# The last pass of a three-way product in 64-row halves, two chunks at a time, in the expert stage of a vision block

## What is computed

```python
logits = jnp.einsum('td,ed->te', xt, router_w)
probs = jax.nn.softmax(logits, axis=-1)
topk_w, topk_idx = jax.lax.top_k(probs, TOP_K)
topk_w = topk_w / jnp.sum(topk_w, axis=-1, keepdims=True)
comb = comb.at[jnp.arange(T)[:, None], topk_idx].add(topk_w)
for e in range(NUM_EXPERTS):           # 16 experts, 8 of width 128, 8 of width 256
    h = jax.nn.gelu(xt @ w1[:, off:off + wd])
    out = out + comb[:, e:e + 1] * (h @ w2[off:off + wd, :])
```

## Time and profile before

| | us |
|---|---|
| median of three runs | 736.07 |
| the profiled execution | 739.34 |
| its span in the trace | 737.6 |
| PE busy | 680.3 |
| VectorE busy | 496.5 |
| ScalarE busy | 356.3 |
| GpSimd busy | 108.2 |

### The profile page before, as it was taken

The page is one execution under the profiler, slowest core; times in us unless marked ns, Lnnn a source line. Parts: engine busy times, 40 slices in busy tenths (PEclk is TensorE's granted clock), DMA queues, the critical chain, the costliest instruction groups (busy, mean ns, idle before and its releaser), DMA issues.

```text
span 737.6 us, 30455 instructions
## 1 busy us (share of the span) xinstructions
PE 680.3 (92%) x13218; PEld 595.5 (81%) x13218; DVE 496.5 (67%) x1354; ACT 356.3 (48%) x921; POOL 108.2 (15%) x328
## 2 busy tenths in 40 slices
PE   5668999999999999999999999869999999999996
PEld 2457888788888888888888878748898898998986
DVE  5257778777878878877778877447456546646644
ACT  0125664655655655555555655534334344434432
POOL 0122123123123123223123211110000000000000
PEclk9969999999999999999999999979999999999999
DMA  8951111011011011111000000000000000000000
GB/s 311 300 182 60 61 48 44 33 44 48 33 60 33 32 60 32 32 61 32 32 4 5 4 4 4 4 1 2 1 1 21 0 0 21 0 0 21 0 0 22
DMA packets 12244, 30.48 MB, mean 41 GB/s; under 512 B 1120, under 2 KB 7392, under 8 KB 11616
## 3 DMA queue, kind: packets, MB, share of 16 engines
q1 hardware_dynamic: 12128, 28.73, 11.9%
HBM read 27.16 MB, written 1.57 MB: 39 GB/s over the span
## 4 chain that ended last, share of the span: by engine, by line
PE 76%; DVE 14%; ACT 5%; issue 3%; DMA 1%; POOL 1%; DVEq 0%; ACTq 0%; SPq 0%; POOLq 0%
PE ps L364 24%; PE ps L493 17%; PE ps L484 15%; PE ps L263 6%; DVE uu L734 3%; DVE sq L653 2%; PE ps L277 2%; PE ps L382 2%; PE ps L314 2%; DVE rf L741 2%; ACT qq L557 2%; PE ps L448 2%; PE ps L278 1%; ACT rr L561 1%; PE ps L375 1%
## 5 line engine op out<-in xcount | busy, mean ns | idle before, releaser
L884 DVE SCALAR_TENSOR_TENSOR acc<-ps,comb,acc 128x192 f32 x256 | 89.2, 411 | 90.3 <-PE ps L493 90.3
L493 PE MATMUL ps<-w_sb,work 128*128 128x192 f32 x768 | 139.9, 326 | 0.5 <-ACT work L633 0.3
L364 PE MATMUL ps<-rr 64*64 64x64 f32 x3840 | 131.4, 221 | 6.0 <-issue 3.3
L493 PEld LDWEIGHTS ps<-w_sb,work 128*128 128x128 f32 x768 | 129.2, 189 | 9.5 <-issue 1.7
L364 PEld LDWEIGHTS ps<-rr 64*64 64x64 f32 x3840 | 119.8, 136 | 18.7 <-ACT rr L561 10.6
L557 ACT ACTIVATE qq<-ps 128x384 f32<-128x384 f32 x192 | 92.3, 490 | 66.7 <-PE ps L364 64.7
L734 DVE SCALAR_TENSOR_TENSOR uu<-rr,qq 128x384 f32<-128x384 f32 x160 | 87.9, 559 | 50.8 <-ACT qq L557 44.6
L633 ACT ACTIVATE work<-ps 128x512 f32<-128x512 f32 x96 | 57.3, 597 | 133.6 <-PE ps L484 133.6
L561 ACT ACTIVATE rr<-ps 128x384 f32<-128x384 f32 x160 | 73.9, 490 | 80.6 <-PE ps L364 79.8
L364 PE MATMUL ps<-uu,qq 64*64 64x64 f32 x4608 | 96.6, 224 | 16.1 <-DVE uu L734 13.9
L364 PEld LDWEIGHTS ps<-uu,qq 64*64 64x64 f32 x4608 | 80.6, 134 | 33.9 <-DVE uu L734 30.6
(11 more groups left out here) (136 smaller groups left out, 1026.8 us busy)
## 6 DMA issues: line engine op xcount, KB each, us to landing
xtb<-xt_dram SPq DMA_DIRECT2D x16, 512.0 KB, 3.5
work<-x_dram SPq DMA_DIRECT2D x16, 512.0 KB, 3.4
wsh<-ws_dram SPq DMA_DIRECT2D x2, 1440.0 KB, 7.8
w_sb<-w_dram SPq DMA_DIRECT2D x1, 2304.0 KB, 26.3
w_a<-w_dram SPq DMA_DIRECT2D x1, 1536.0 KB, 13.2
w_b<-w_dram SPq DMA_DIRECT2D x2, 768.0 KB, 17.7
out_dram<-acc SPq DMA_DIRECT2D x4, 384.0 KB, 2.7
mult<-copies_dram SPq DMA_DIRECT2D x1, 512.0 KB, 12.8
```

Of the source, the lines that this page charges most:

```text
L364: last = pe.matmul(ps[z:z + 64, 2 * lane + i, 64 * j:64 * j + 64], lhs[r, lane, i, j, :], rhs[r, lane, i, j, :], start=True, stop=True)
L493: last = pe.matmul(ps[:, 2 + 2 * (e % 2) + j // 2, (j % 2) * DIM:(j % 2 + 1) * DIM], hid[:, c % 4, j * P:(j + 1) * P], w2_sb[:, c, :], sta ...
L884: last = dve.scalar_tensor_tensor(out=a, in0=ps[:, 2 + 2 * (e % 2) + j // 2, (j % 2) * DIM:(j % 2 + 1) * DIM].unsqueeze(1), scalar=comb[:, ...
```

## The change

Chunks are numbered through all groups, n from 0 to 95, and the loops over groups are written out on all engines. PE takes chunks in pairs. For a pair, `up_full` makes the first four passes of n, then of n + 1; then `up_half` makes the fifth pass of each on 64 rows: rows 0 to 63 for an even n, rows 64 to 127 for an odd one. The half used is the one where `wb` still holds the high part, so `low_part` now overwrites rows 64 to 127 for an even n and 0 to 63 for an odd one. The fifth pass has so far also had low part by xlo on the other half; this product is no longer computed. PE's order is up_pair(0), then up_pair(n + 2), down(n), down(n + 1). The up banks are three, 6, 0 and 1 (`UPB`); the weight slots are four (`SLOTS`), filled four chunks ahead; the memory for them comes from `wsh` and `whalo`, which only the start of the kernel uses. ACT's order per pair is two gelus, then two `high_part`; DVE's is two `low_part`, then the adds of the experts that end in the pair. `high_part` and `low_part` of four chunks instead of two stand ahead of `iteration(16)`.

```diff
+FIRST = [sum(WIDTH[:e]) for e in range(EXPERTS)]
+EXPERT_OF = [e for e in range(EXPERTS) for _ in range(WIDTH[e])]
+NC = NT // GT * HID
+UPB = (6, 0, 1)
+SLOTS = 4
...
-        wah, wal, wb = (sb(n, [P, 3, P], F32R) for n in ("wah", "wal", "wb"))
+        with nc.sbuf_tensor("wsh", [P, 2, 5, 3, DIM], F32) as wsh, nc.sbuf_tensor("whalo", [P, 2, DIM], F32) as whalo:
+            pass
+        wah, wal, wb = (sb(n, [P, SLOTS, P], F32R) for n in ("wah", "wal", "wb"))
...
+            def up_full(n):
+                g = n // HID
+                pe.wait_ge(whi_ready, 2 * n + 2)
+                pe.wait_ge(wlo_ready, 2 * n + 2)
+                if n >= 3:
+                    pe.wait_ge(gelu_done, n - 2)
+                tok4, k = slice(g * GT * P, (g + 1) * GT * P), n % SLOTS
+                parts = ((wah, xhi, 0), (wah, xlo, 0), (wal, xhi, 0), (wb, xhi, 1))
+                for m, (w, xs, half) in enumerate(parts):
+                    pe.matmul(ps[:, UPB[n % 3], :], w[:, k, :], xs[:, half, tok4], start=(m == 0), stop=False)
+
+            def up_half(n):
+                g, r = n // HID, slice(64 * (n % 2), 64 * (n % 2) + 64)
+                tok4 = slice(g * GT * P, (g + 1) * GT * P)
+                pe.matmul(ps[:, UPB[n % 3], :], wb[r, n % SLOTS, :], xlo[r, 1, tok4], start=False, stop=True).then_inc(up_done, 1)
+
+            def up_pair(n):
+                up_full(n)
+                up_full(n + 1)
+                up_half(n)
+                up_half(n + 1)
...
+            up_pair(0)
+            for n in range(0, NC, 2):
+                if n + 2 < NC:
+                    up_pair(n + 2)
+                down(n)
+                down(n + 1)
...
             act.wait_ge(ffw_loaded, 64)
-            high_part(0)
-            high_part(1)
+            for n in range(4):
+                high_part(n)
             iteration(NT)
...
+            for n in range(0, NC, 2):
+                gelu(n)
+                gelu(n + 1)
+                for m in (n + 4, n + 5):
+                    if m < NC:
+                        high_part(m)
...
-            low_part(0, 0)
-            low_part(0, 1)
+            for n in range(4):
+                low_part(n)
             iteration(NT)
...
+            for n in range(0, NC, 2):
+                for m in (n + 4, n + 5):
+                    if m < NC:
+                        low_part(m)
+                for m in (n, n + 1):
+                    g, c = divmod(m, HID)
+                    e = EXPERT_OF[c]
+                    if c == FIRST[e] + WIDTH[e] - 1:
+                        add_expert(g, e)
```

More of the change, by code:

```diff
@@ L184, in _ @@
                 tile_loads(t)
-            with sp.Fori(0, NT // GT) as g:
+            for g in range(NT // GT):
                 sp.wait_ge(expert_added, (g + 1) * EXPERTS + 2)
-                sp.dma_start(out[bass.ds(g * GT, GT)].rearrange("t p n -> p t n"),
-                             acc[:, bass.ds(g * GT, GT), :]).then_inc(out_stored, 16)
+                sp.dma_start(out[g * GT:(g + 1) * GT].rearrange("t p n -> p t n"),
+                             acc[:, g * GT:(g + 1) * GT, :]).then_inc(out_stored, 16)
             sp.wait_ge(out_stored, 16 * (NT // GT))
@@ L471, in _ @@
             pe.wait_ge(lexp, NT)
[L472 to L504, removed]
@@ new lines, in up_half, with down @@
+            def up_half(n):
[7 more added lines that the diff above has]
+                up_half(n + 1)
+            def down(n):
+                g, c = divmod(n, HID)
+                e = EXPERT_OF[c]
+                if c == FIRST[e]:
+                    pe.wait_ge(expert_added, g * EXPERTS + e + 1)
+                pe.wait_ge(gelu_done, n + 1)
+                for j in range(GT):
+                    last = pe.matmul(ps[:, 2 + 2 * (e % 2) + j // 2, (j % 2) * DIM:(j % 2 + 1) * DIM],
+                                     hid[:, n % 4, j * P:(j + 1) * P], w2_sb[:, c, :],
+                                     start=(c == FIRST[e] and j % 2 == 0), stop=(c == FIRST[e] + WIDTH[e] - 1),
+                                     skip_group_check=True)
+                if c == FIRST[e] + WIDTH[e] - 1:
+                    last.then_inc(down_done, 1)
@@ L618, in _, with high_part, gelu @@
                 iteration(t)
-            def high_part(c):
+            def high_part(n):
+                c = n % HID
                 for w, raw in ((wah, w1_a), (wb, w1_b)):
-                    act.activation(w[:, c % 3, :], raw[:, c % HID * P:(c % HID + 1) * P], ACT.Copy).then_inc(whi_ready, 1)
+                    act.activation(w[:, n % SLOTS, :], raw[:, c * P:(c + 1) * P], ACT.Copy).then_inc(whi_ready, 1)
+            def gelu(n):
+                act.wait_ge(up_done, n + 1)
+                if n >= 4:
+                    g, c = divmod(n - 4, HID)
+                    act.wait_ge(down_done, g * EXPERTS + EXPERT_OF[c] + 1)
+                act.activation(hid[:, n % 4, :], ps[:, UPB[n % 3], :], ACT.Gelu_apprx_tanh).then_inc(gelu_done, 1)
             act.wait_ge(ffw_loaded, 64)
-            high_part(0)
-            high_part(1)
+            for n in range(4):
+                high_part(n)
             iteration(NT)
[L627 to L635, removed]
+            for n in range(0, NC, 2):
[4 more added lines that the diff above has]
+                        high_part(m)
         @block.vector
@@ L857, in _, with low_part, add_expert @@
                 iteration(t)
[L859 to L863, removed]
[L864 removed]
+            def low_part(n):
+                dve.wait_ge(whi_ready, 2 * n + 2)
+                k, col = n % SLOTS, n % HID * P
+                for w, high, raw, r in ((wal, wah, w1_a, slice(0, P)), (wb, wb, w1_b, slice(64 * (1 - n % 2), 64 * (1 - n % 2) + 64))):
+                    dve.tensor_tensor(w[r, k, :], raw[r, col:col + P], high[r, k, :].bitcast(F32),
+                                      ALU.subtract).then_inc(wlo_ready, 1)
+            def add_expert(g, e):
+                dve.wait_ge(down_done, g * EXPERTS + e + 1)
+                dve.wait_ge(expert_added, g * EXPERTS + e + 2)
+                for j in range(GT):
+                    a = acc[:, g * GT + j, :]
+                    last = dve.scalar_tensor_tensor(
+                        out=a, in0=ps[:, 2 + 2 * (e % 2) + j // 2, (j % 2) * DIM:(j % 2 + 1) * DIM],
+                        scalar=comb[:, g * GT + j, e:e + 1], in1=a, op0=ALU.mult, op1=ALU.add)
+                last.then_inc(expert_added, 1)
             dve.wait_ge(ffw_loaded, 64)
[L866 to L867 removed]
+            for n in range(4):
+                low_part(n)
             iteration(NT)
```

2 lines of the change are left out of this document (removed).

## The result

The changed kernel takes 740.10 us (median of 6 runs, 739.20 to 740.84) against 736.27 for the kernel before (6 runs, 735.48 to 738.45): a ratio of 1.0047, with a 95% interval of 1.0032 to 1.0062. It is slower by half a per cent. The forecast was 740.4, slower; for the profiled execution it was 743.6, and that one took 739.53, so the 3.3 us by which the profiled execution of before stood above its median did not carry over.

The account below looks back on a forecast made before the run. TensorE was taken to bound the expert stage. Switches +7.2, seams and late low parts -3.1 and before the stage +0.2 sum to +4.3 on a median of 736.07: 740.4 us, range 729.5 to 746 (8 in 10).

Parts of the forecast that it names:

- The switches: Expert stage: two tile-shape changes per pair cost 0.40, halves streaming together save 0.22; 0.15 net per pair, +7.2 us.
- the open 0.02: Each switch: 0.02 of a 0.23 pass isn't streaming and may run beside the drain; lower end +0.14 per pair.
- Rival B: Switches: no drain between the two shapes, loads hidden; a pair saves 0.22, 722.6 us; chance 0.11.
- C: Switches: the drain stays but the weight loads go under it; -0.07 per pair, 729.8 us; chance 0.05.
- D: Switches: the load is hidden at one switch only; 0.04 per pair, 735.1 us; chance 0.07.
- E: Fifth passes: the halves don't run together and save nothing; a pair costs 0.22 more, 751.0 us; chance 0.08.
- Seams and late low parts: Expert stage: group seams (1.5) and VectorE's late low parts (1.6) go; -3.1 us, or only -1.5.
- Before the stage: VectorE's queue ahead of the last norm: two more low parts take 1.25 against 1.02 idle, +0.2 us; ScalarE's conversions nothing.
- The tail: After the last down product: the same as before, no change in time.

Follow-up runs that it names:

- experiment 3: The changed kernel with each half right behind the full passes of its own chunk, four switches of shape per pair: 772.80 us, ratio 1.0497.
- experiment 2: The changed kernel with both halves on rows 0 to 63, so that they can't stream together: 753.24 us, ratio 1.0231.
- Experiment 1: The changed kernel with the fifth pass back on all 128 rows; pairs, three banks, four slots and written-out loops stay: 731.45 us, 0.9936 of the kernel before.
- experiment 5: The kernel before with only the loops over groups written out; single chunks, full fifth passes, two banks, three slots: 730.81 us, ratio 0.9937.
- experiment 10: The kernel before with only VectorE's expert loop written out, constants in place of registers: 733.35 us, ratio 0.9975.
- experiment 9: The changed kernel with the halves of four chunks behind each other, four up banks, eight slots, run a second time: 729.69 us, ratio 0.9922.
- experiment 4: The changed kernel without any fifth pass, so no switch of shape is left: 709.38 us, ratio 0.9635.
- experiment 6: The changed kernel with the halves of four chunks behind each other, four up banks, eight slots, first run: 729.77 us, ratio 0.9919.
- experiment 8: The changed kernel with four chunks at a time, four up banks, eight slots, but full fifth passes on 128 rows: 731.02 us, ratio 0.9939.
- second profile of before: The kernel before, unchanged, profiled once more: 734.79 us, span 733.0, expert stage 241.0 us.

## Why the prediction was right

**The switches** (+7.2, from 6.7 to 8.6). The pair costs 0.167 more than with full fifth passes, 8.0 us; 0.15 had been taken between 0.14 and 0.18. The terms: 0.19 into the halves and 0.20 back, against 0.20 each; the drain of 0.09 and the bare load of 0.11, both read from other shapes, hold for 64*128 within 0.01. It was the choice nearer to the lower end that was off; whether the open 0.02 runs beside the drain can't be told from this. By experiment 3 the price is 0.20 into a half and 0.21 out of it, for the first as for the second half, and by experiment 2 the second half is nearly free only on other rows.

**Rival B** (no drain), **C** and **D** (hidden loads) are out by the timeline: the first half's load comes 0.31 after the last full pass, not 0.23, and each switch costs 0.19 to 0.21, with the load in it. **E** is out by experiment 2. The Trainium skill's sentence that a change of the tiling mode drains the TensorE (TensorEngine Tiling (Array Packing), Key Properties) agrees: the 0.31 are a pass of 0.23 and 0.08 to 0.09 in which nothing starts. The Trainium skill's span model (TensorE: Matmul & The Clock Gate, Measured speedup vs the span model) gives a packed group one matmul plus about 4 ns per further tile. The trace agrees for the second half, which starts under 0.01 us after the first; the model leaves out the two switches around the group, and they are nine tenths of a pass each.

**Seams and late low parts** (-3.1). Experiment 1 against the kernel before has 237.0 us in the stage for 240.8: -3.8. The step was right in sign and a fifth too small. Experiments 1 and 5 split the 3.8: written-out loops give 2.6 (the seams 1.6, the late low parts and the first chunks the rest), where 3.1 had been taken, and the order in pairs gives 1.2, to which the prediction gave nothing: it took 4.92 for a pair, and it is 4.90 where single chunks make 4.927. The account of the late low parts was wrong: I gave them to the depth of two chunks and their cure to the four slots. Experiments 5 and 10 cure them with three slots. Experiment 10 takes all register instructions out of VectorE's loop; those ahead of the adds are the ones that delay anything, 0.2 us, since those ahead of the low parts run while an add still does. They were to be seen in the trace of before, as the distance between the last down's end and the add.

**Before the stage** (+0.2). Not borne out in the changed kernel. Eight low parts took from 477.60 to 479.77, 2.17 us for 1.25: 0.92 more where 1.25 had been taken, and that fits into the 1.02 of idle time. ScalarE's four conversions fit as forecast: of its idle 1.84, 1.03 are left. The norm's wait of 0.82 for PE says little, since PE's four products ahead of it ran at half the clock in that profile (1.63 us for 0.92). At full clock, experiment 9, with the same low parts, has

```profile
478.67 0.92 PE L389 MATMUL ps<-wp_sb,ot 128*128 128x192 f32 x4 [0.53 <-ACT ot L582]
...
479.24 0.28 DVE L886 TENSOR_TENSOR wb<-w_b,wb 64x128 fp32r<-64x128 f32 x1
479.62 0.36 DVE L772 TENSOR_TENSOR acc<-ps,acc 128x192 f32<-128x192 f32 x1
```

and experiment 1

```profile
480.77 0.92 PE L389 MATMUL ps<-wp_sb,ot 128*128 128x192 f32 x4 [0.53 <-ACT ot L583]
...
481.70 0.29 DVE L885 TENSOR_TENSOR wb<-w_b,wb 64x128 fp32r<-64x128 f32 x1
482.02 0.36 DVE L771 TENSOR_TENSOR acc<-ps,acc 128x192 f32<-128x192 f32 x1
```

In 9 the norm follows PE at once; in 1 it starts 0.33 after PE's last record, right behind the last low part. The difference is in the rows that `low_part` overwrites. Where they alternate (the changed kernel, experiments 3, 4, 6 and 9) eight low parts take 2.15 to 2.17 us; where they are always 64 to 127 (1, 2 and 8) they take 2.53, and then the 1.25 - 1.02 of the prediction is right in kind, with 0.3 for 0.2. From the start of the attention's last output products to the first up are 9.00 us in experiments 5, 6 and 9, and 9.31 and 9.29 in 1 and 8.

The prediction had nothing for the entry into PE's own loop. Before, the first up starts 0.57 after the router's exponential ends, and 0.21 in the changed kernel; from the norm to the first up are 7.24 us in the three profiles in which PE loops (before twice, and experiment 10), and 6.87 to 6.88 in all others. That gains 0.36.

**The tail** ("the same") was wrong by some 0.9 us. The second profile of before has 5.34 us from the last down's end to the span's end, the changed kernel and experiments 1, 5 and 6 have 4.5. 0.2 is the register work before the last adds, and 0.2 more are SP's register instructions between the adds and the store (733.44 to 733.65, where the changed kernel has 734.67 to 734.70). The rest is the landing of the last store. In the second profile of before and in experiment 10 that store is (KB, us from issue to landing)

```profile
out_dram<-acc SPq DMA_DIRECT2D x1, 384.0 KB, 3.1
...
out_dram<-acc SPq DMA_DIRECT2D x1, 384.0 KB, 2.6
```

and in the first profile of before 3.5. Experiment 10 keeps the store's loop with its address from registers, and the first three stores of before land in 2.6 to 2.7 with such addresses. Experiment 9 has one of 3.2 with a constant address. So the address is not what made the last store longer; what did stays open.

The sum: the changed kernel's stage is +5.0. Of it the switches are +8.0, the loops and the pairs -3.8, and the remaining 0.8 fits a clock at half for 5.2 us into the stage, where experiment 1 and the kernel before have 3.4; the other kernels lie between 3.4 and 6.1 us, and I take that for chance, without having shown it. The way to the stage is +0.35: +0.7 for PE's products at half clock in that profile, -0.36 for PE's loop. With the tail, -1.3 against the first profile of before and -0.9 against the second, that makes +4.1 and, with the 241.0 of the second profile's stage, +4.2, against 3.8 measured by the medians. Forecast less measured, the errors of the terms are -0.8 for the switches, +0.7 for loops and pairs, +0.9 for the tail, +0.2 for the low parts and +0.4 for PE's loop, and -1.5 for the clock, for which no term stood. They nearly cancel. So the sign and the main term were foreseen, and it is luck that the 740.4 lies as near to 740.1.

## What to carry to other kernels

- Packing two half-height products beside each other saves a pass, but going into the other tile shape and back cost 0.39 us here: the drain of the array and a weight load with nothing over it, twice. So more must be packed per switch: one pass of 0.23 saved per two switches lost 8 us in all, two passes saved per two switches gained 1.3.
- A change that does two things must be measured as two. Writing the loops out gained 4.6 us by itself, and hid more than half of what the halves lost; the version with only that, or with four chunks per switch (729.7), beats both kernels.
- In an engine's hand-written loop, look at the distance between the end of what it waited for and its next instruction: 0.2 us of register work there moved a wait onto the bound engine.

## What the hardware showed unexpectedly

- VectorE's low parts alternate between a subtraction on all 128 partitions and one on 64. Where the latter is on rows 64 to 127 each time, eight take 2.53 us (experiments 1, 2, 8); where every other one is on rows 0 to 63, 2.16 (the changed kernel, 3, 4, 6, 9), with some of the starts 0.2 apart in place of 0.3.
- Register instructions before a store put 0.2 us between the last add and its issue (before, experiment 10), against 0.03 with a constant address.
- A lone half on 64 rows and 512 columns takes as long as two beside each other, 0.42 to 0.43 with its switch; its stream is 0.23, like a full pass.
- Alternating single ups and downs costs 0.013 us per chunk more than pairs (4.927 against 4.900 per pair in experiments 5 and 1), though the profile of either shows no wait in the middle of the stage.
